# Reordering the first scores of each attention group, and leaving out the identity products

## The reference

```
Q, K, V = x @ W_q, ctx @ W_k, ctx @ W_v           (16 heads of 8)
attn    = softmax(Q K^T / sqrt(8))                (per batch and head, 256 x 256)
out     = (attn V) @ W_o + b_o
```

## Time and profile before

| | us |
|---|---|
| median of 3 runs | 210.16 |
| the profiled execution | 208.93 |
| its span | 207.2 |
| PE busy | 179.9 (87%) |
| DVE busy | 141.6 (68%) |
| ACT busy | 102.9 (50%) |

### The profile page before, as it was taken

How to read it: one execution, slowest core, us unless ns; L and a number is a source line. 1 busy time by engine, 2 the same in 40 slices (tenths; PEclk the granted TensorE clock), 3 DMA queues, 4 the chain that set the end, 5 groups by cost and what they waited for, 6 DMA issues and landing times.

```text
span 207.2 us, 3930 instructions
## 1 busy us (share of the span) xinstructions
PE 179.9 (87%) x1410; PEld 141.7 (68%) x1410; DVE 141.6 (68%) x404; ACT 102.9 (50%) x184; POOL 36.8 (18%) x52
## 2 busy tenths in 40 slices
PE   5699899899999999999999999788878887889331
PEld 4389598678799988888888887545556654557210
DVE  2899758667467556746455958669778867875684
ACT  2266478444423222532336225966785587547243
POOL 3734274624000000400000003500000000004400
PEclk9979999999999999999999999999999999999955
DMA  6993000000000000000000000000000000000002
GB/s 200 391 413 126 5 2 0 0 3 0 0 0 5 0 0 3 0 0 0 3 0 0 0 5 0 0 3 0 5 0 0 3 3 2 0 3 2 0 0 101
DMA packets 3330, 6.61 MB, mean 32 GB/s; under 512 B 880, under 2 KB 2160, under 8 KB 3056
## 3 DMA queue, kind: packets, MB, share of 16 engines
q1 hardware_dynamic: 1440, 5.51, 6.8%
q10 hardware_dynamic: 1872, 0.87, 1.5%
HBM read 5.84 MB, written 0.52 MB: 31 GB/s over the span
## 4 chain that ended last, share of the span: by engine, by line
PE 71%; DVE 15%; issue 5%; ACT 3%; POOL 3%; DMA 1%; DVEq 0%; POOLq 0%; ACTq 0%
PE banks L1126 12%; PE bank L1197 7%; PE bank L1162 6%; PE bank L948 6%; PE bank L950 5%; PE bank L949 5%; DVE negm L798 4%; PE banks L1184 3%; PE bank L1170 3%; PE banks L949 2%; PE banks L948 2%; PE banks L950 2%; PE bank L1206 2%; PE bank L1126 2%; POOL rstd L246 2%
## 5 line engine op out<-in xcount | busy, mean ns | idle before, releaser
L798 DVE TENSOR_REDUCE negm<-bank 128x2 f32<-128x512 f32 x60 | 39.6, 688 | 14.2 <-PE bank L1162 13.9
L456 ACT ACTIVATE raw<-banks 128x1024 f32<-128x1024 f32 x32 | 31.0, 1020 | 22.3 <-PE banks L1184 22.3
L419 ACT ACTIVATE att<-bank 128x512 f32<-128x512 f32 x32 | 19.1, 598 | 45.3 <-PE bank L950 32.6
L1162 PE MATMUL bank<-stk 32*128 32x256 f32 x120 | 22.3, 313 | 0.2 <-DVE negm L798 0.2
L777 DVE SCALAR_TENSOR_TENSOR xs<-banks,rw,xs 128x128 f32<-128x128 f32 x56 | 15.8, 344 | 7.8 <-PE banks L1126 7.7
L1162 PEld LDWEIGHTS bank<-stk 32*128 32x128 f32 x120 | 14.5, 183 | 9.2 <-issue 7.9
L948 PE MATMUL bank<-xT,w 128*128 128x512 f32 x48 | 20.1, 420 | 0.5 <-DVE xT L706 0.5
L1126 PEld LDWEIGHTS banks<-raw,attT 128*128 128x128 f32 x160 | 19.2, 192 | 1.2 <-issue 0.5
L1126 PE MATMUL banks<-raw,attT 128*128 128x128 f32 x160 | 19.7, 276 | 0.0
L950 PE MATMUL bank<-xT,w 128*128 128x512 f32 x48 | 18.8, 392 | 0.0
L244 POOL TENSOR_SCALAR vpe<-mv 128x4 f32<-128x4 f32 (+1 forms) x9 | 2.4, 268 | 92.4 <-DVE mv L575 92.2
(11 more groups left out here) (202 smaller groups left out, 371.0 us busy)
## 6 DMA issues: line engine op xcount, KB each, us to landing
raw<-in_w SPq DMA_DIRECT2D x1, 2048.0 KB, 10.4
raw<-in_w SPq DMA_DIRECT2D x1, 1024.0 KB, 9.2
xs<-in_x SPq DMA_DIRECT2D x2, 256.0 KB, 3.2
ctxT<-in_ctxT SPq DMA_DIRECT2D x1, 512.0 KB, 5.3
ctx<-in_ctx SPq DMA_DIRECT2D x1, 512.0 KB, 6.4
wl<-in_wl SPq DMA_DIRECT2D x1, 256.0 KB, 7.2
picks<-in_sel ACTq DMA_DIRECT2D x1, 256.0 KB, 11.5
out<-cT SPq DMA_DIRECT2D x1, 256.0 KB, 2.1
```

Source lines behind the costliest of these rows:

```text
L419: act.activation(silus[:, k, :], bk[2 * k][:, :], ACT.Silu).then_inc(S["silu_s"], 1)
L456: act.activation(probs[:, m % 2, 2 * r:2 * r + 2, :, :].rearrange("p h k q -> p (h k q)"), pair[r][:, :], ACT.Exp, scale=ATT_SCALE).then_i ...
L798: dve.tensor_reduce(negm[:, m % 2, :, c0:c0 + 1].rearrange("p t c -> p (t c)"), bk[score_bank(m, r)][:, :].rearrange("p (t k) -> p t k", t ...
L1162: ins = pe.matmul(bk[score_bank(m, r)][:, t * SEQ:(t + 1) * SEQ], stk[rows, m % G, t * P:(t + 1) * P], stk[rows, m % G, SEQ:2 * SEQ], star ...
```

## The change

`score_bank`: the scores of group m go to bank `1 + (m + r) % 2`, so that neighbours in r are in different banks; `scores(0, 3)` goes to bank 1 instead of 6.

PE: in the last unit of the expert layer `scores(0, 2)` and `scores(0, 3)` are both issued ahead of `down(13)`. `scores(m + 1, 0)` is issued in group m behind `turn_maxima(m)` (up to group 2) or behind `bank7_used(m)` (later), where before it was issued at the end of group m - 1. `shifted_scores(m)` comes next, ahead of `scores(m + 1, 1)` and `pick_group(m + 3)`. `scores(m + 1, 3)` stays behind `outputs(m - 1)` from group 1 on. In group 0 `down(14)` and `down(15)` stand between the scores of group 1, and `pick_group(3)` behind them.

DVE: `shifted(m)` comes ahead of `maxima(m + 1, 0)`. `weigh(13)` and `weigh(15)` move into groups 0 and 1, behind `maxima(m + 1, 0)`, and `weigh(14)` behind `maxima(1, 2)`. `queries_lo`, `add_attention` and `normalise` now stand between `maxima(m + 1, 1)` and `maxima(m + 1, 2)`.

ACT: in group 2 the exponentials stand ahead of `third_scaled`.

The identity products of groups 0, 1, 2, 7 and 11 are left out (23 calls of `keep_warm`'s product); those at the end stay.

```diff
-WARMED = {1: 3, 2: 3, 2 * G - 1: 2, 3 * G - 1: 2}
         def score_bank(m, r):
             if m == 0:
-                return 6
-            return 2 - m % 2 if r == 2 else 1 + m % 2
+                return 6 if r < HPG - 1 else 1
+            return 1 + (m + r) % 2
...
+                exps(m, 0)
+                exps(m, 1)
                 if m == 2:
                     for t in range(*HALVES[1]):
                         third_scaled(t)
-                exps(m, 0)
-                exps(m, 1)
...
             def dve_group(m):
+                shifted(m)
                 if more:
                     maxima(m + 1, 0)
-                shifted(m)
+                if m < 2:
+                    weigh(UNITS - 3 + 2 * m)
+                if more:
+                    maxima(m + 1, 1)
                 if m == G:
                     queries_lo(1)
...
                 if 0 < b < BATCH - 1 and g == 2:
                     normalise(b - 1, 1)
                 if more:
-                    maxima(m + 1, 1)
+                    maxima(m + 1, 2)
                 if m == 0:
                     weigh(UNITS - 2)
-                if more:
-                    maxima(m + 1, 2)
-                if m == 0:
-                    weigh(UNITS - 1)
...
-                if n >= 2:
+                if 2 <= n < UNITS - 1:
                     weigh(n - 2)
...
             def scores(m, r):
                 pe.wait_ge(S["stack_s"], m + 1)
-                if m == 0:
+                if m == 0 and r == HPG - 1:
+                    pe.wait_ge(S["hid_s"], HB * (UNITS - 1) + 1)
+                elif m == 0:
                     pe.wait_ge(S["s1_max"], r)
                 elif r == 0:
-                    pe.wait_ge(S["s1_max"], 4 * m - 1)
-                elif r == 2:
+                    pe.wait_ge(S["hid_s"], HB * UNITS)
+                    pe.wait_ge(S["s1_max"], 4 * m)
+                elif r == 1:
                     pe.wait_ge(S["qa_s"], m)
                 else:
-                    pe.wait_ge(S["s1_max"], 4 * m + (r + 1) // 2)
+                    pe.wait_ge(S["s1_max"], 4 * m + r - 1)
...
-                if m in WARMED:
-                    pe.wait_ge(S["p_s"], 2 * m - 1)
-                    keep_warm(3, WARMED[m])
...
                 turn_maxima(m)
+                if more and m < 3:
+                    scores(m + 1, 0)
+                if m == 0:
+                    down(UNITS - 2)
                 if not final:
                     bank7_used(m)
+                if more and m >= 3:
+                    scores(m + 1, 0)
+                shifted_scores(m)
                 if more:
                     scores(m + 1, 1)
                 if 0 < m < GROUPS - 3:
                     pick_group(m + 3)
-                shifted_scores(m)
                 if more:
                     scores(m + 1, 2)
                 if m == 0:
                     down(UNITS - 1)
+                if more:
+                    scores(m + 1, 3)
+                if m == 0:
                     pick_group(3)
-                    pe.wait_ge(S["p_s"], 1)
-                    keep_warm(3, 4)
                 if m >= 1:
                     bank7_free(m)
                     outputs(m - 1)
-                if more:
-                    scores(m + 1, 3)
-                if m == 0:
-                    keep_warm(3, 4)
-                if m + 2 < GROUPS:
-                    scores(m + 2, 0)
-                if m == 1:
-                    pe.wait_ge(S["p_s"], 3)
-                    keep_warm(3, 5)
...
                 if n >= UNITS - 2:
                     scores(0, 2 * (n - UNITS + 2))
+                if n == UNITS - 1:
+                    scores(0, HPG - 1)
                 down(n - 2)
                 if n == 3:
                     logits(1)
-                if n >= UNITS - 2:
-                    scores(0, 2 * (n - UNITS + 2) + 1)
-            pe.wait_ge(S["hid_s"], HB * UNITS)
-            scores(1, 0)
-            down(UNITS - 2)
+                if n == UNITS - 2:
+                    scores(0, 1)
```

## The result

The changed kernel takes 226.03 us (median of 4 runs, 221.9 to 232.8). Against the kernel before on the same chip the ratio is 1.060, 95% interval 1.050 to 1.071: slower. The ratio leaves out runs far above the fastest; the changed kernel's runs differ by 5%, and the reason is itself a finding, TensorE's clock. The profiled execution took 223.69 us, with a span of 221.9, against 208.93 and 207.2 before.

A forecast was written before the change was run, and what follows sets the result against it. The prediction took the order of hand-overs between PE and DVE as the bound. Groups 4 to 14 at +9.4 us less 1.15 at the head made +8.3, lifting the median from 210.16 to 218.5 us, range 214 to 225.

The forecast's parts named there:

- The held product: In attention groups, DVE holds the values' product until a time D; the next group starts at D + 2.35 us.
- The seven held groups: Groups 5, 6, 9, 10 would take 5.57 us, 8 and 12 5.41, group 4 6.12, the values' product waiting for DVE.
- Group 13's sum: Nothing holds the product, but normalise lies ahead of the last two maxima: 3.22 + 1.29 + 0.04 = 4.55 us against 4.14.
- Groups 4 to 14 by the order: Summed lengths of these attention groups: 56.9 us against 47.5 before, so +9.4 us.
- Groups 7 and 11: These attention groups wait for ACT's copy, lose two identity products and gain the first scores: 4.35 us against 4.48.
- the new alternation of banks: Neighbouring pairs of scores would overlap, 0.2 us each in groups 0, 7 and 11; median 217.9; weighed, left out.
- The head: Start of the attention stage: group 1 starts 2.8 us earlier, part given back, leaving -1.15 us at group 4.
- pay little here: 15 of the 23 identity products had DVE's or ACT's work beside them, so removing them gains little.
- Rival B: TensorE's clock falls in the held groups, about 1.1 us a fall; four falls give 223, eight 227; 35%.
- A: Main case: DVE holds the values' product in seven groups, less the head's gain; 218.5 us, range 216 to 220.5; 50%.
- C: The values' product is not held; the seven groups take 4.1 to 4.3 us (group 4 5.0), total 209.3; 7%.
- D = 2.1: Time after a group's start that decides C: DVE releasing the values' product before its turn; forecast had 3.06 to 3.77.

The follow-up runs named there:

- e9: Changed kernel with scores(m + 1, 3) behind outputs(m - 1) from group 1 on; 249.2 us, ratio 1.185.
- e3: Changed kernel with queries_lo, add_attention and normalise directly behind shifted(m) instead of behind maxima(m + 1, 1); 230.2 us, ratio 1.093.
- e5: Changed kernel with identity products in PE's waits, and ACT's stacked(m + 3) ahead of o_copy(m - 1); 219.6 us.
- e1: Changed kernel with the 23 identity products put back; 225.8 us.
- e2: Kernel before with only the 23 identity products left out and nothing moved; 214.69 us, ratio 1.021.
- e11: Kernel before with only the change's head, and identity products in groups 2 to 15 only where PE waits; 207.31 us, ratio 0.985.
- e12: Kernel before with the same fill of PE's waits as e11 and its own head; 209.81 us, ratio 0.997.
- e10: Changed kernel with scores(m + 1, 0) ahead of bank7_used in every group, no fill; 244.1 us, ratio 1.158.

## Why the prediction was right in its direction and off in its steps

- **The held product: wrong for this kernel.** "Queued behind the waiting product on PE are the last scores of the group" was a misreading of the diff. With those scores ahead of it, the product comes to its turn only when DVE has let go of bank 7, and it waits for nothing in groups 5, 6, 8 and 9 and for about 0.1 in group 4. The seven held groups take 4.57 to 4.65 (group 4: 5.32) at full clock, not 5.41 to 5.57 (6.12). e9 shows the mechanism, at half clock, in the order for which I had worked it out.
- **Group 13's sum was the right one for groups 5, 6, 9 and 10.** With DVE's file as the end I had 4.55 there; they took 4.57 to 4.64. That a second path, over the product and its copy, is as long (e3) I had not seen. Group 13 itself comes to 5.6 at full clock, since "nothing holds the product" overlooked the wait for `stacked(15)` (e5: 0.5 us, and 1.6 for the fall that came with it). Groups 4 to 14 by the order: +4.9 instead of +9.4.
- **Groups 7 and 11: right.** At full clock and without identity products such a group takes 4.35 (e3), as forecast; e1 has 4.67 with two of them in it. The 0.2 us that I had weighed for the new alternation of banks did not come off it. **Groups 8 and 12** have 4.65 in place of 5.41; in 8 the chain has the copy of the product, which now ends a group, and bank 7's next work waits for it.
- **The head: right, and its gain real.** The turn of group 1 came 3.0 us earlier (12.3 behind the last up-projection's start, 15.3 before), forecast 2.8. The four group lengths at full clock give -1.1 at group 4, forecast -1.15. What I had wrong is that the other 15 identity products "pay little here": without them the clock fell in group 1 (0.69 in e2), with them it did not (e1).
- **Rival B came, beside A.** I had given 35% to a falling clock and priced a fall at 1.1 us; in this execution the clock was low for 34 us in six stretches, two of them three times as long as the others, and by the estimate above they cost 9.3. That is about 0.27 us for each us at the low level, so my 1.1 for some 3 us was near; the number of falls and their length were not. A had 218.5, B 223 for four falls; the median is 226, and the ratio times the 210.16 of before 222.8. B's evidence (PE half idle at 8:10, then 0.50) was the right row, but it does not tell when: in the changed kernel's own execution PE was busy for the same 0.97 of 2 us in 8:10, and the clock in 10:12 was 1.00. The Trainium skill (TensorE: Matmul & The Clock Gate, HAM oscillation) ties falls to waits longer than any here. The trace disagrees: the first fall, at 124.6, came 0.5 us into a wait of 1.16 us, and no other wait of PE in the groups is longer.
- **C, the product not held: right that the product is not held, wrong in its time.** It decided at "D = 2.1", but the product itself now comes later, at 3.44 after the turn (147.35). Two paths then end a group at 4.6 where C had 4.1 to 4.3.

That the size came near was luck: the held product made the order 4.5 us too dear, and A had left out 9.3 us of clock.

## What to carry to other kernels

Read the new order of each queue out of the whole new function, not out of the diff's lines: which instruction is last before the wait decides whether a wait costs anything. Before taking out work that only fills a wait, price the clock without it, and put such work into waits that end later anyway (e11: two identity products in group 5, still 4.01; in group 4, where two more stood on PE's way, 5.51 for 5.01). And split a reordering: here the head was worth -2.5 us (e11 against e12), and groups 4 to 14 cost an estimated 4.9 at full clock before the clock took its part.

## What the runs showed of the hardware that I had not expected

- The clock can stay low under load. In e9 it was at 0.50 from 140 to 200 us with PE busy 52.3 of 60, and in e10 with 58.1 of 60. At half clock the busy share is high because the products are long, so busy time does not tell whether the clock will rise.
- One set of scores issued elsewhere (e9, e10) cost 23 and 18 us against the changed kernel. In e9 the estimate at full clock explains some 6 of them (seven groups by 0.9); the rest is put down to the clock.
- The same program is at full clock in one execution and not in the next: the kernel before took 209.0 to 240.5 us over 17 executions, with a mean granted clock of 0.98 to 0.79. What decides it no run here shows.
